# A four-layer graph network: group sums in four PSUM banks, turned rows stored from ScalarE's queue, x copied by rank beside the rank loop

## The chip, the cores and the metric

The kernel runs on 1 core of one Trainium2 chip. The time is device microseconds of one execution, as a median of runs. All numbers are fp32 unless said otherwise.

## The reference

50000 nodes with 128 features, 50000 edges sorted by `dst`. Four residual layers, each on `h = relu(layernorm(x))`:

```python
dst = (50000 * uniform ** 2.0), sorted        # a few nodes get many edges
# layer 0: two graph convolutions
h1 = relu(segsum((h * ns @ W1)[src], dst) * nd + b1)
x  = x + segsum((h1 * ns @ W2)[src], dst) * nd + b2
# layer 1: x + [h, mean_in(h)] @ W.T + b
# layer 2: SAGE: h4 = relu(h @ Ws1 + mean_in(h) @ Wn1 + b1); x + h4 @ Ws2 + mean_in(h4) @ Wn2 + b2
# layer 3: m = gelu([h[src], h[dst], ew] @ We1 + be1) @ We2 + be2
#          u = gelu([h, segsum(m, dst)] @ Wu1 + bu1) @ Wu2 + bu2; x + layernorm(h + u) * gamma + beta
```

`ns`, `nd` are roots of the degrees, `mean_in` is the mean over a node's incoming edges.

## The kernel before

**Setup.** The 50000 nodes are 392 blocks of 128, the edges 392 tiles of 128. A histogram gives degrees and the edges of each block. The blocks are ranked by rising number of edges; four ranks make a group, 98 groups. The rank loop (98 turns) places the edges by rank of their block: TensorE counts, VectorE reads out positions, GpSimd scatters four times a turn. Beside it the first layer's table is made: SyncE loads 512 rows of x into `XB` (`load0`), ScalarE norms them into `HO`, TensorE turns them, ScalarE copies them (`HT`), TensorE multiplies by W1, ScalarE copies the product (`T1`), SyncE stores it (`store0`).

**Walks.** Then come six walks over the edges (`walk(ph)`, ph 0 to 5), one for each segment sum. A walk has 784 steps in 98 windows of 8; a step multiplies one tile of gathered messages (`M`, a ring of 32 tiles of 128 rows, filled by GpSimd's indirect gathers, four tiles a chunk) with a one-hot matrix (`OH`, VectorE compares `lane` with `dstrel`) and adds it to the sums of one block in PSUM. Steps go on to the next block or the next tile, as the data has it; tables `tab_p` (TensorE: rows and sums of each step, banks to clear), `tab_a` (ScalarE: banks to copy and slots in `AG`) and `tab_w` (GpSimd: the window that frees a chunk) say which. The sums of three groups stand in banks 0 to 2. A window first clears the banks that become new (two matmuls by zero, also into unused banks 4 and 6 where none does), after ScalarE has copied the sums of the window before (`ev_act`). After a window ScalarE copies two banks to `AG`.

**Consumers.** Beside each walk the finished groups are processed, some windows later: rows scaled and x added (VectorE, `pre`), variance, deviation (ScalarE), scale and offset (`coefficients`), norm to `HO` (ScalarE), transposed by TensorE into `pt` (bank 3), copied to `HT`, multiplied (banks 4, 5 or 6, 7 by parity), copied to `T1`, the state added to `T2`, and both stored as the next walk's table and state. After walk 2 the turned rows are stored too (`h3_d`), after walk 4 (`h5_d`) as well; walk 3 has a two-layer network as its consumer. Walk 5 gathers by src and by dst from a table of pairs, makes the messages (gelu), stores them and loads them back in order, and its consumer makes the output. Walks 0 to 5 are the first to the sixth walk in the prediction.

**Order.** Each engine runs `staggered(...)`: in step n it does part (lag, do) for group n - lag, in the order of the list, so each list is the order written out by hand of one engine's queue. Waits block everything behind them in that list. The second convolution's x is needed in rank order: `placed1` (SyncE, walk 0) stores four blocks of the table and copies four blocks of x from DRAM to DRAM for each group. In code:

```python
staggered(sp, [(3, store0), (1, rows_for(s_ho))])                       # rank loop, SyncE
staggered(sp, [(5, placed1)])                                           # walk 0, SyncE
staggered(act, [(5, product(1)), (4, turned(1)), (3, normed(1, Z)), (0, sums(0))])
staggered(dve, [(0, onehots(1)), (4, coefficients(2, s_pre)), (6, added(2, ...)), (3, pre(2, ndr, b2bc))], chain, 4)
staggered(dve, [(0, onehots(2)), (4, coefficients(3, s_pre)), (3, pre(3, rdr, lbbc))], chain, 4)
```

`link` makes VectorE wait for its own last operation.

Of the kernel before, what the change touches and what calls it, by code (L numbers as in the profile page):

```python
# [57 lines left out]
class Chain:  # L58
# [15 lines left out]
    def link(self, ins):  # L74
        ins.then_inc(self.sem, 1)
        if self.i is None:
            self.done += 1
            self.eng.wait_ge(self.sem, self.done)
        else:
            self.k += 1  # L80
            self.eng.wait_ge(self.sem, self.i * self.per + (self.done - self.first * self.per + self.k))
# [27 lines left out]
def program(nc, a, out):  # L109
    with ExitStack() as ctx, ExitStack() as early:  # L110
# [32 lines left out]
        def four(t):  # L143
# [56 lines left out]
        bb_i = tmp("bb_i", [1, WINS], I32); b12_i = tmp("b12_i", [1, STEPS], I32); t16 = tmp("t16", [1, WINS], I32)  # L200
        b12_f = tmp("b12_f", [1, STEPS]); g_f = tmp("g_f", [1, WINS]); gk = tmp("gk", [1, 3, WINS]); gw = tmp("gw", [1, 3, WINS])
        g3_i = tmp("g3_i", [1, 3, WINS], I32); g3_f = tmp("g3_f", [1, 3, WINS]); moved = tmp("moved", [1, WINS]); spare = tmp("spare", [1, WINS]); fresh = tmp("fresh", [1, 2, WINS]); high = tmp("high", [1, WINS], I32)
        p_f = tmp("p_f", [1, STEPS]); m_f = tmp("m_f", [1, STEPS])
# [12 lines left out]
        AG = sb("AG", [P, AGR * W4])  # L216
# [8 lines left out]
        pt = ps[3]  # L225
# [16 lines left out]
        ev_act = sem("sums_copied")  # L242
# [6 lines left out]
        s_mma = sem("hidden_products"); s_hid = sem("hidden_made"); s_z6 = sem("updated_normed"); s_nrm = sem("updated_scaled"); s_fin = sem("output_made")  # L249
        s_es = sem("edges_summed"); s_gl = sem("messages_made")  # L250
        in_ = pair("rows_loaded"); late = pair("late_loaded")
        st = pair("table_stored"); sv = pair("state_stored"); sh = pair("turned_stored")
# [4 lines left out]
               "mma": [0, 0, 0, 0, 1, 0, 1], "hid": [0, 0, 0, 0, 1, 0, 1]}  # L257
        TURN = {"in": [64, 0, 32, 16, 16, 16, 32], "late": [0, 0, 0, 0, 16, 0, 16], "st": [16, 64, 64, 64, 64, 64, 64],
                "sv": [0, 64, 16, 16, 16, 16, 0], "sh": [0, 0, 0, 16, 0, 16, 0]}
# [36 lines left out]
        def half_of(d, b, k):  # L296

            if d == 4:
                return [ps[4 + 2 * h].rearrange("p (j k d) -> p j k d", j=2, k=2)[:, :, k, :] for h in range(2)]
            return [banks[:, (4 + 2 * b) * W4:(6 + 2 * b) * W4].rearrange("p (j k d) -> p j k d", j=Q4, k=2)[:, :, k, :]]  # L300
# [12 lines left out]
        def _(sp):  # L313
# [62 lines left out]

            staggered(sp, [(1, rows_for(s_var))])
# [11 lines left out]

            def spots(g):  # L390

                return entries(sp, tab_s[0:1, ds(g * Q4, Q4)], Q4, (BLOCKS - 1) * P)
# [11 lines left out]
            def whole_rows(d, table, buf, ready, done):  # L404

                def do(i, b):
                    g = 2 * i + b
                    sp.wait_ge(ready[0], g + (at(d, ready[1]) + 1))
                    stand(sp)
                    sp.dma_start(table[g], buf[:, b, :]).then_inc(done[b], 16)  # L410
# [16 lines left out]
            def placed1(i, b):  # L427
                g = 2 * i + b
                sp.wait_ge(s_t1, g + (at(1, "t1") + 1))
                stand(sp)  # L430
                to = spots(g)
                for j, r in enumerate(to):
                    sp.dma_start(tabs[1][ds(r, P), :], q(T1[:, b, :])[:, j, :]).then_inc(st[b], 16)
                for j, r in enumerate(to):
                    if isinstance(g, int) and g == GROUPS - 1 and j >= 2:
                        part = slice((j - 2) * (REST // 2), (j - 1) * (REST // 2))
                        sp.dma_start(q(x_rank[g])[part, 2, :], rest(2)[part]).then_inc(sv[b], 16)
                        continue
# [591 lines left out]
        def _(dve):  # L1030
# [305 lines left out]
            def pre(d, col, bias):  # L1336

                def do(i, b):
# [10 lines left out]
                    if d == 2:  # L1349
                        stand(dve)  # L1350
# [93 lines left out]
```

## Time and profile before

| | |
|---|---|
| median of 3 runs (lowest to highest) | 5862.01 us (5845.89 to 5865.06) |
| profiled execution | 5851.2 us, span 5849.4 us |
| granted TensorE clock, mean | 0.911 |
| busy: TensorE, VectorE, ScalarE, GpSimd | 4302.6, 3428.6, 3079.0, 3264.7 us |
| DMA | 879 MB, mean 150 GB/s |

Stages from the first gather or scatter of one to that of the next: setup to 441 us, rank loop to 1079, tables to 1157, then the walks to 1791, 2458, 3051, 4015, 4658 and the end. In rows of the profile PE is TensorE, PEld its weight loads, DVE VectorE, ACT ScalarE, POOL GpSimd, SP SyncE, `<-` names what ended an idle time. The clock is a share of the full 2.4 GHz. fp32 matmuls show two records each.

### The profile page before, as it was taken

The numbers are of one execution on the slowest core, as the hardware profiler recorded it, in microseconds if no ns is written. First come the engines' busy times: TensorE is split into PE (matmuls) and PEld (weight loads), VectorE is DVE, ScalarE is ACT, GpSimd is POOL, SyncE is SP. The second block draws the span as 40 slices with busy tenths as digits, with TensorE's granted clock in tenths as the row PEclk, the third lists the DMA queues.
The fourth block names the chain that finished last, engine by engine and source line by source line (L and its number), as shares of the span: only waits on it lengthen the run. The fifth ranks groups of instructions, "written<-read, shape, count | busy, mean of one in ns | idle before, by whom it ended". The sixth has DMA issues, their size and how long they took to land. (4 is left out here: it accounts for less than half of the span.)

```text
span 5849.4 us, 136722 instructions
## 1 busy us (share of the span) xinstructions
PE 4302.6 (74%) x23129; PEld 3083.8 (53%) x23130; DVE 3428.6 (59%) x11290; ACT 3079.0 (53%) x6571; POOL 3264.7 (56%) x3244
## 2 busy tenths in 40 slices
PE   4556666577766888666649999998888537777777
PEld 1123333265555666555537777776667425455554
DVE  6875555443335877688843333334777426666666
ACT  7954444155545666466633333334666416666667
POOL 0006555275775557676764333454667577777771
PEclk8879999699988999889869999999999769999998
DMA  2212333144444555477754444455888646666665
GB/s 76 75 50 77 81 83 80 42 122 123 131 125 130 154 158 165 138 242 235 240 153 129 132 134 134 142 149 157 252 254 262 188 117 188 188 194 189 187 190 146
DMA packets 1061001, 879.24 MB, mean 150 GB/s; under 512 B 134328, under 2 KB 866000, under 8 KB 1060924
## 3 DMA queue, kind: packets, MB, share of 16 engines
q1 hardware_dynamic: 960572, 697.60, 39.5%
q0 software_dynamic: 100352, 180.83, 12.0%
q14 instruction: 56, 0.46, 0.0%
q8 instruction: 21, 0.34, 0.0%
HBM read 491.13 MB, written 412.40 MB: 154 GB/s over the span
## 5 line engine op out<-in xcount | busy, mean ns | idle before, releaser
L965 PE MATMUL banks<-M,OH 128*128 x9408 | 1322.5, 300 | 291.8 <-POOLq L593 167.4
L564 POOL DMA_INDIRECT M<-table_a,six x1176 | 1244.1, 1058 | 520.6 <-issue 327.5
L965 PEld LDWEIGHTS banks<-M,OH 128*128 128x128 f32 x9408 | 1246.0, 211 | 460.9 <-issue 432.0
L564 POOL DMA_INDIRECT M<-table_b,six x784 | 787.4, 1004 | 728.3 <-PE banks L965 499.6
L653 ACT ACTIVATE AG<-banks x1176 | 633.6, 591 | 771.6 <-PE banks L965 765.3
L1311 DVE TENSOR_TENSOR OH<-lane,dstrel 128x1024 f32<-128x1024 f32 x588 | 719.9, 1225 | 479.0 <-PE banks L965 348.4
L559 POOL DMA_INDIRECT edges_by_block<-pack,pos_i x392 | 376.0, 959 | 690.5 <-DVE pos_i L1184 591.5
L956 PE MATMUL banks<-zero_h 128*128 128x512 f16 x1176 | 360.8, 389 | 411.9 <-issue 254.6
L653 ACT ACTIVATE T<-banks 128x512 f32<-128x512 f32 (+1 forms) x588 | 295.9, 520 | 534.9 <-DMA table_b<-T 229.3
L883 PE MATMUL banks<-ident,HO 128*128 128x128 f32 x2352 | 380.8, 286 | 210.8 <-ACT HO L670 173.7
L564 POOL DMA_INDIRECT M<-table_pairs,dix x392 | 446.9, 1140 | 119.5 <-issue 101.8
L564 POOL DMA_INDIRECT M<-table_pairs,six x392 | 377.5, 963 | 128.2 <-issue 114.0
L653 ACT ACTIVATE HT<-banks 128x512 f32<-128x512 f32 x686 | 407.0, 593 | 57.1 <-PE banks L883 50.2
L883 PEld LDWEIGHTS banks<-ident,HO 128*128 128x128 f32 x2352 | 280.4, 145 | 294.4 <-ACT HO L670 192.1
L956 PEld LDWEIGHTS banks<-zero_h 128*128 128x128 f16 x1176 | 114.1, 97 | 572.8 <-issue 548.6
L1361 DVE TENSOR_TENSOR T<-banks,XB 128x256 f32<-128x256 f32 x196 | 74.0, 419 | 566.5 <-ACT T L653 559.3
L1002 PE MATMUL banks<-w,H 128*128 128x256 f32 x1568 | 355.1, 380 | 5.9 <-ACT H L762 5.9
L674 ACT ACTIVATE HO<-Z,BI,SC 128x128 f32<-128x128 f32 x784 | 322.3, 483 | 64.9 <-DVE BI L1268 58.7
L1177 DVE CUSTOM_DVE_ANT_0 junk<-banks,oh_bk 128x392 f32<-128x392 f32 x392 | 220.2, 562 | 218.3 <-PE banks L871 213.7
L670 ACT ACTIVATE HO<-XB,dclamp,steps_c 128x128 f32<-128x128 f32 x392 | 161.3, 482 | 336.1 <-DMA XB<-in_x 322.8
L1392 DVE SCALAR_TENSOR_TENSOR ES<-we1c,ewT,M 128x128 f32<-128x128 f32 x392 | 111.6, 346 | 356.1 <-POOLq L593 295.8
L1002 PEld LDWEIGHTS banks<-w,H 128*128 128x128 f32 x1568 | 290.4, 190 | 44.6 <-ACT H L762 9.2
(270 smaller groups left out, 7795.8 us busy)
## 6 DMA issues: line engine op xcount, KB each, us to landing
XB<-state SPq DMA_DIRECT2D x392, 256.0 KB
state<-T SPq DMA_DIRECT2D x196, 256.0 KB
table_a<-T SPq DMA_DIRECT2D x784, 64.0 KB
state<-Z SPq DMA_DIRECT2D x196, 256.0 KB
h_turned<-HT SPq DMA_DIRECT2D x196, 256.0 KB
table_pairs<-T SPq DMA_DIRECT2D x392, 128.0 KB
M<-messages SPq DMA_DIRECT2D x98, 512.0 KB, 4.2
XB<-in_x SPq DMA_DIRECT2D x390, 128.0 KB
```

The lines of the kernel that those rows point to most:

```text
L559: nc.gpsimd.indirect_dma_start(out=edges, out_offset=bass.IndirectOffsetOnAxis(ap=pos_i[b][:, j:j + 1], axis=0), in_=pack[b][:, j, :], in_ ...
L564: nc.gpsimd.indirect_dma_start(out=M[:, slot, :], out_offset=None, in_=table, in_offset=bass.IndirectOffsetOnAxis(ap=idx, axis=0)).then_in ...
L653: return nc.scalar.activation(dst_, src_, ACT.Copy)
L670: last = nc.scalar.activation(q(HO[:, b, :])[:, j, :], cell, ACT.Relu, bias=bix[:, ds(g * Q4 + j, 1)], scale=scx[:, ds(g * Q4 + j, 1)])
L674: last = nc.scalar.activation(q(HO[:, b, :])[:, j, :], cell, ACT.Relu, bias=BI[:, b, j:j + 1], scale=SC[:, b, j:j + 1])
L883: last = nc.tensor.transpose(q(pt)[:, j, :], q(src_[:, b, :])[:, j, :], ident[:, :])
L956: mm(banks[:, ds(fresh_at[k], W4)], zero_h[:, 0:P], zero_h[:, :], start=True, stop=False, skip_group_check=True)
L965: last = mm(banks[:, ds(sums_at[k], P)], OH[:, b * US + k, :], source[:, ds(rows_at[k], P)], start=False, stop=False, skip_group_check=True)
L1002: last = mm(half, q(H[:, b, h, :])[:, j, :], w42[:, h, :, :].rearrange("p k d -> p (k d)"), start=(h == 0), stop=(h == 1))
L1177: v.tensor_tensor_reduce(junk[:, c % 2, :], ps[4 + c % 2][:, 0:BLOCKS], oh_bk[:, c, :], 1.0, 0.0, ALU.mult, ALU.add, posf[:, c:c + 1]).the ...
L1311: v.tensor_tensor(OH[:, b * US:(b + 1) * US, :], lanes, ids, ALU.is_equal).then_inc(oh_ready, 1)
L1392: last = v.scalar_tensor_tensor(q(ES[:, b, :])[:, j, :], we1c[:, :], ewT[:, ds(c * GC + j, 1)], M[:, b * GC + j, :], ALU.mult, ALU.add)
```

## The change

1. *Four banks.* Sums stand in banks 0 to 3. `tab_p` clears one bank ahead of a window and one ahead of its fifth step; the first clear waits for the copies of the window before the last, the second for the first copy of the last window (`ev_first`). `AG` gets a spare slot for copies that carry nothing. `pt` moves to bank 4, products to banks 5 and 6 for both parities, the fourth walk's to 7 and 4, and the wait `copied` of the walks goes.
2. *Constants in PSUM.* Bank 7 holds `lane` and the biases b1, b2 and that of layer 1; one-hots of walks 0, 1, 2 and 4 and the bias adds read them there.
3. *x by rank.* `by_rank` copies x in the rank loop, four blocks a turn; walk 0 has the table's stores alone.
4. *Turned rows* of walks 2 and 4 are stored from ScalarE's queue.
5. *VectorE's consumer* is split in six parts (`walked`), rows of walks 1, 2 and 4 are scaled into four slots (`Z4`), the bias is added a step before it is used.
6. *Walk 5.* ScalarE makes `T1`; norm, gamma and beta are 12 operations 128 wide on VectorE instead of ScalarE's four and VectorE's three 512 wide.
7. Other orders and lags in nearly every list, and shorter table arithmetic ahead of the walks.

```diff
-        pt = ps[3]
+        pt = ps[4]
+        lanes_p, b1_p, b2_p, lb_p = (ps[7][:, k * P:(k + 1) * P] for k in range(4))
 # SyncE
-            staggered(sp, [(3, store0), (1, rows_for(s_ho))])
+            def by_rank(i, b):
+                g = 2 * i + b
+                for j, r in enumerate(spots(g)):
...
+                    sp.dma_start(q(x_rank[g])[:, j, :], a["x"][ds(r, P), :]).then_inc(sx[b], 16)
+            staggered(sp, [(1, rows_for(s_ho)), (4, store0), (4, by_rank)])
-            staggered(sp, [(5, placed1)])
+            staggered(sp, [(0, placed(1, tabs[1], T1, (s_t1, "t1"), st))])
 # ScalarE
+                    act.dma_start(table[g], HT[:, b, :]).then_inc(sh[b], 16)
-                    copy(AG[:, ds(spot[2], W4)], banks[:, ds(spot[0], W4)])
+                    copy(AG[:, ds(spot[2], W4)], banks[:, ds(spot[0], W4)]).then_inc(ev_first, 1)
                     copy(AG[:, ds(spot[3], W4)], banks[:, ds(spot[1], W4)]).then_inc(ev_act, 1)
-            staggered(act, [(5, product(1)), (4, turned(1)), (3, normed(1, Z)), (0, sums(0))])
+            staggered(act, [(0, sums(0)), (2, turned(1)), (1, normed(1, Z)), (3, product(1))])
-            staggered(act, [(5, product(2)), (4, turned(2)), (3, normed(2, None)), (0, sums(1)), (2, deviations(...))])
+            staggered(act, [(4, normed(2, None)), (1, sums(1)), (4, turned(2)), (5, product(2)), (3, deviations(...))])
-            staggered(act, [(4, turned(3)), (3, normed(3, Z)), (0, sums(2)), (2, deviations(...))])
+            staggered(act, [(1, sums(2)), (3, deviations(...)), (5, turned(3)), (3, normed(3, None)), (5, turned_stored(3, h3_d))])
 # TensorE, products
-                    need(pe, s_t1, g + (at(d, "t1") - 1))
+                    need(pe, s_t1, g + at(d, "t1") - (1 if d < 2 else 0))
 # TensorE, walk
-                    need(pe, ev_act, w + WINS * ph)
-                    for k in range(2):
-                        mm(banks[:, ds(fresh_at[k], W4)], zero_h[:, 0:P], zero_h[:, :], ...)
+                    need(pe, ev_act, w + (WINS * ph - 1))
+                    mm(banks[:, ds(fresh_at[0], W4)], zero_h[:, 0:P], zero_h[:, :], ...)
...
                     for k in range(US):
+                        if k == US // 2:
+                            need(pe, ev_first, w + WINS * ph)
+                            mm(banks[:, ds(fresh_at[1], W4)], zero_h[:, 0:P], zero_h[:, :], ...)
-            staggered(pe, [(0, walk(3, copied(4, 5))), (4, out4), (2, turn_rows(4, HO)), (3, hidden4)])
+            staggered(pe, [(0, walk(3)), (2, turn_rows(4, HO)), (3, hidden4), (4, out4)])
 # VectorE
-                    lanes = lane[:, :]...
+                    lanes = (lanes_p if ph in (0, 1, 2, 4) else lane[:, :])...
-            staggered(dve, [(0, onehots(1)), (4, coefficients(2, s_pre)), (6, added(2, ...)), (3, pre(2, ndr, b2bc))], chain, 4)
+            staggered(dve, [(5, roots), (5, offsets), (4, summed_rows), (4, stats), (4, variances), (0, onehots(1)), (3, biased), (6, added(2, ...))], chain, 3)
-            staggered(dve, [(0, onehots(2)), (4, coefficients(3, s_pre)), (3, pre(3, rdr, lbbc))], chain, 4)
+            staggered(dve, [(4, summed_rows), (4, stats), (4, variances), (0, onehots(2)), (3, biased), (4, roots), (4, offsets)], chain, 3)
 # VectorE, final of walk 5
-                link(v.tensor_tensor(q(XB[:, b, :]), q(XB[:, b, :]), four(bet), ALU.add))
-                link(v.tensor_tensor(q(T2[:, b, :]), q(HO[:, b, :]), four(gam), ALU.mult))
-                v.tensor_tensor(T2[:, b, :], T2[:, b, :], XB[:, b, :], ALU.add).then_inc(s_fin, 1)
+                for j in range(Q4):
+                    v.tensor_tensor(q(XB[:, b, :])[:, j, :], q(XB[:, b, :])[:, j, :], bet[:, :], ALU.add)
+                for j in range(Q4):
+                    last = v.scalar_tensor_tensor(q(T2[:, b, :])[:, j, :], q(Z[:, b, :])[:, j, :], MV[:, b, j, 0:1], gam[:, :], ALU.subtract, ALU.mult)
+                for j in range(Q4):
+                    last = v.scalar_tensor_tensor(q(T2[:, b, :])[:, j, :], q(T2[:, b, :])[:, j, :], SC[:, b, j:j + 1], q(XB[:, b, :])[:, j, :], ALU.mult, ALU.add)
-            staggered(dve, [(0, edges6), (L + 6, updated), (L - 1, onehots(5)), (L + 7, coefficients(6, s_z6)), (L + 2, pre6), (L + 8, final)], chain, 6)
+            staggered(dve, [(0, edges6), (L + 6, updated), (L - 1, onehots(5)), (L + 7, final)], chain, 4)
```

## Rows read from the trace of the kernel before

**Rows 1.** Windows by stage: length, busy PE, PEld, DVE, ACT, POOL, clock, DMA, GB/s.

```profile
441.00:1079.00 638.00, 422.42 (x2338) 252.24 (x2337) 358.49 (x1552) 265.43 (x584) 376.02 (x392) 0.92 0.31 81
1157.00:1791.00 634.00, 444.88 (x2943) 356.94 (x2943) 229.41 (x489) 316.63 (x784) 419.45 (x405) 0.94 0.45 121
1791.00:2458.00 667.00, 522.72 (x2943) 423.86 (x2943) 510.38 (x1668) 388.28 (x882) 416.12 (x405) 0.92 0.52 155
2458.00:3051.00 593.00, 371.80 (x2159) 296.27 (x2159) 439.04 (x1567) 342.88 (x784) 416.70 (x405) 0.85 0.71 216
3051.00:4015.00 964.00, 942.47 (x4511) 682.92 (x4511) 316.50 (x490) 342.86 (x686) 380.91 (x405) 0.99 0.46 133
4015.00:4658.00 643.00, 504.70 (x2940) 416.80 (x2941) 449.86 (x1568) 386.77 (x882) 421.46 (x406) 0.93 0.80 240
4658.00:5850.00 1192.00, 826.04 (x4314) 557.67 (x4312) 745.20 (x2058) 705.41 (x1174) 828.75 (x808) 0.89 0.59 173
```

**Rows 2.** Windows, steady stretches of four walks, L965 alone (PE, PEld).

```profile
1250.00:1650.00 400.00, 138.76 (x1065) 126.12 (x1063) 0.99 0.48 128
1900.00:2400.00 500.00, 180.74 (x1216) 166.86 (x1216) 0.93 0.54 160
2500.00:2900.00 400.00, 180.53 (x1183) 166.32 (x1182) 0.91 0.78 238
4100.00:4500.00 400.00, 146.69 (x1047) 135.04 (x1048) 0.96 0.85 255
```

**Rows 3.** GpSimd's groups: busy, mean ns, idle before; first, second, third, fifth, sixth walk.

```profile
L564 POOL DMA_INDIRECT M<-table_a,six x392 | 414.4, 1057 | 180.2 <-issue 110.9 <-PE banks L965 57.3 <-POOL six L573 9.5
L564 POOL DMA_INDIRECT M<-table_b,six x392 | 409.9, 1046 | 220.3 <-issue 108.3 <-PE banks L965 103.0 <-POOL six L573 7.5
L564 POOL DMA_INDIRECT M<-table_a,six x392 | 412.3, 1052 | 155.3 <-issue 107.7 <-PE banks L965 30.6 <-POOL six L573 10.3
L564 POOL DMA_INDIRECT M<-table_a,six x392 | 417.4, 1065 | 185.1 <-issue 108.9 <-PE banks L965 63.8 <-POOL six L573 9.4
L564 POOL DMA_INDIRECT M<-table_pairs,dix x392 | 446.9, 1140 | 119.5 <-issue 101.8 <-DMA M<-table_pairs,dix 12.2 <-DMA M<-table_pairs,six 5.5
```

**Rows 4.** Timeline, three places: start us, length us, engine, instruction.

```profile
4309.88 1.22 DVE L1311 TENSOR_TENSOR OH<-lane,dstrel 128x1024 f32<-128x1024 f32 x1 [0.34 <-issue]
...
4310.02 1.90 POOL L564 DMA_INDIRECT M<-table_a,six  x1 [0.30 <-issue]
...
5209.66 0.67 DVE L1413 TENSOR_TENSOR XB<-XB,bet 128x512 f32<-128x512 f32 x1
...
5209.80 1.35 POOL L564 DMA_INDIRECT M<-table_pairs,dix  x1 [0.30 <-issue]
...
3507.62 0.76 DVE L1361 TENSOR_TENSOR T<-banks,XB 128x256 f32<-128x256 f32 x2 [6.15 <-ACT T L653]
3507.74 0.95 POOL L564 DMA_INDIRECT M<-table_b,six  x1 [0.30 <-issue]
```

**Rows 5.** Timeline of the rank loop and of SyncE's queue in the first walk.

```profile
763.07 0.93 SPq L366 DMA_DIRECT2D XB<-in_x  x2
...
766.70 1.65 ACT L670 ACTIVATE HO<-XB,dclamp,steps_c 128x128 f32<-128x128 f32 x4 [3.59 <-DMA XB<-in_x]
...
1604.56 2.90 SPq L440 DMA_DIRECT2D x_by_rank<-in_x  x4
```

**Rows 6.** Timeline of VectorE, one step of the second walk.

```profile
2105.05 1.23 DVE L1311 TENSOR_TENSOR OH<-lane,dstrel 128x1024 f32<-128x1024 f32 x1 [0.33 <-issue]
...
2106.79 0.69 DVE L1361 TENSOR_TENSOR T<-banks,H 128x512 f32<-128x512 f32 x1 [0.23 <-issue]
2107.40 0.72 DVE L1342 TENSOR_TENSOR XB<-XB,b2bc 128x512 f32<-128x512 f32 x1
2108.76 1.14 DVE L1323 SCALAR_TENSOR_TENSOR H<-AG,ndr,XB 128x128 f32 x4 [0.65 <-ACT HO L674]
...
2111.39 1.23 DVE L1311 TENSOR_TENSOR OH<-lane,dstrel 128x1024 f32<-128x1024 f32 x1
```

More of the change, by code:

```diff
@@ L77, in link, with made, after @@
             self.done += 1
[L78 to L81, printed above, removed]
+            return self.done
+        self.k += 1
+        return self.i, self.per, self.done - self.first * self.per + self.k
+    def made(self, less):
+        if self.i is None:
+            return self.done - less
+        return self.i, self.per, self.done - self.first * self.per + self.k - less
+    def after(self, mark):
+        if not isinstance(mark, int):
+            mark = mark[0] * mark[1] + mark[2]
+        self.eng.wait_ge(self.sem, mark)
+    def link(self, ins):
+        self.after(self.mark(ins))
 def staggered(eng, parts, chain=None, links=0):
@@ L425, in kept @@
                     sp.wait_ge(sems[k], turns(d + 1, what))
[L427 to L438, printed above, removed]
-                    r = nc.s_assert_within(r, 0, (FULL - 1) * P, skip_runtime_bounds_check_because="the last two ranks are the last two blocks")
-                    sp.dma_start(q(x_rank[g])[:, j, :], a["x"][ds(r, P), :]).then_inc(sv[b], 16)
-            staggered(sp, [(5, placed1)])
-            kept(1, "sv", sv)
+            staggered(sp, [(0, placed(1, tabs[1], T1, (s_t1, "t1"), st))])
+            for k in range(2):
+                sp.wait_ge(sx[k], 64 * TURNS)
             def load2(i, b):
                 g = 2 * i + b
-                need(sp, s_var, g + (at(2, "var") - 1))
+                need(sp, s_row, g + (at(2, "row") - 1))
                 stand(sp)
@@ L996, in out4 @@
                 pe.wait_ge(s_hid, g + (at(4, "hid") + 1))
+                pe.wait_ge(s_ht, g + (at(4, "ht") + 3) if not isinstance(g, int) else at(4, "ht") + min(g + 3, GROUPS))
                 need(pe, s_t1, g + at(4, "t1"))
@@ L1302, in _, with constants @@
             dve.wait_ge(s_tq, 17)
+            def constants():
+                for row, what in ((lanes_p, lane), (b1_p, b1bc), (b2_p, b2bc), (lb_p, lbbc)):
+                    last = v.tensor_copy(row, what[:, :])
+                link(last)
             def onehots(ph):
@@ L1345, in do @@
-                    if d in (3, 5):
-                        need(dve, sv[b], turns(d, "sv", i))
-                    into = Z4(i, b) if d == 2 else Z[:, b, :]
-                    link(scaled(i, b, col, lambda j: q(XB[:, b, :])[:, j, :], into))
-                    if d == 2:
-                        stand(dve)
-                    spread(d, b, into).then_inc(s_var, 1)
-                return do
+                    if bias is None:
+                        dve.wait_ge(in_[b], turns(d, "in", i) + TURN["in"][d])
+                    else:
+                        chain.after(chain.made(0 if isinstance(g, int) else 1))
```

293 lines of the change are left out of this document (153 added, 140 removed).

## The prediction

> **What bounds the kernel now.** I read the table of stages first, then the walks' own matmuls in steady stretches, then GpSimd's gathers, then single steps of the timeline. Outside the setup there are a rank loop and six walks; a walk is 98 windows of 8 steps [rows 1]. Only the fourth walk is full on one engine (TensorE 942 of 964 us). In the others TensorE is busy 372 to 523 us of 593 to 667, so I looked for what paces a window. Sixteen walk matmul records make a window, so a steady window takes 400 x 16 / 1065 = 6.0 us in the first walk, 6.6 in the second, 5.4 in the third and 6.1 in the fifth [rows 2].
>
> GpSimd gathers 392 tiles a walk. A gather that nothing delays takes 0.945 us and the next starts 0.30 later; with some 13 us of table reads, c = 1.26 us a tile. The rows show means of 1.05 to 1.07 and waits for TensorE (the ring of 32 tiles is full) of 57, 103, 31 and 64 us [rows 3]. The timeline shows what lengthens a gather: one that starts 0.14 us into the one-hot comparison ends 0.8 us after the comparison does, 1.90 us in all; the same happens with the 512-wide add of beta; a gather that starts inside an add whose first operand is in PSUM takes 0.95 [rows 4]. The excess over 0.945 is 392 x 0.112 = 44 us in the first walk, 40, 42 and 47 in the second, third and fifth [rows 3].
>
> Both matter because of the data. dst is 50000 u squared and the blocks stand in rising order of edges, so light blocks come first: after w windows N = 392 (1 - v) tiles are used, v = (sqrt(9 - 4w/49) - 1) / 2. Demand rises from 2.7 to 8 tiles a window. A walk at p us a window and c us a tile ends at T = the largest over w of p w + c (360 - N), and not before 98 p or 392 c. Check on before: third walk (p 5.41, c 1.37) 556, fifth (6.1, 1.37) 600, first (6.0, 1.35) 594; the stages are 593, 643 and 634 long [rows 1], so filling and draining add 37 to 43. Where I forecast a walk, the difference of two such T is the gain.
>
> **The change, part by part.** *Rank loop.* Today SyncE's store waits for ScalarE's T copy and stands ahead of the next load, so the load of x is issued at 763.07 and the rows are normed at 766.70, and ScalarE had waited 3.6 us for it; a group takes 638 / 98 = 6.5 us [rows 1, 5]. After, the load stands first and the store lags by 4. The wait falls away, but SyncE gets four copies of x: 2.90 us [rows 5]. Its sum a group: loads 0.93, copies 2.90, and for one store, the gaps and the table read some 1.7: 5.5. GpSimd's four scatters take 4 x 1.26 = 5.0. I take 5.6, and 98 x 0.9 = 88, less 8 for start: **-80**. Bounds: -10 (copies and loads share the queue, the loads land late) and -105 (5.3). Transfers have room: DMA is at 0.31 there.
>
> *Table arithmetic on VectorE* ahead of the walks: 14 us of short one-row operations become some 8: **-6**.
>
> *First walk.* SyncE issues four stores and four x copies a window, 1.9 and 2.9 us plus 1.1 of gaps, which is the 6.0 of the window [rows 2, 5]. The copies leave. What is next: TensorE's own work, 445 / 98 = 4.5 us [rows 1]; the copy of the sums, which held the bank clears, now has a window's slack through the fourth bank and the second half's own wait. I take p = 4.8. One-hot lanes and the bias are read from PSUM, so by rows 4 no gather is delayed: c = 1.26. T = 501 against 594, and two lags less to drain, 8 us: **-102**. Bounds: p 5.5 gives 545, -50; all at GpSimd's 392 x 1.26 = 494 gives -110.
>
> *Second walk.* VectorE is the pace: from one comparison to the next 6.34 us, in it 0.65 us before the scaled rows, spent on ScalarE's norm of two groups back and on register work behind the bias add [rows 6]. Four H slots and the bias add taken a step ahead remove the wait, some 0.25 of register work stays: 5.94. TensorE needs 523 / 98 = 5.3. Products(g) now also wait for both T copies of g - 1. Counted from the start of VectorE's step: those products end at 2.4, ScalarE copies them behind its norm (1.65), sums (1.05) and turned copy (0.6) by 4.3, VectorE adds last in its step by 5.9, and TensorE wants the bank at 6.6: 0.7 to spare. p = 5.94 and c = 1.28 (scaled rows still read two SBUF operands, but 128 wide, about 10 us a walk) give T = 583; before it was 667 less 36 for filling and draining, 631: **-48**. Bounds: 0 and -85 (5.4).
>
> *Third walk.* VectorE's step has the same gap, 5.4 becomes 5.3 (a semaphore wait is added ahead of the statistics, 0.12). ScalarE gets the store of the turned rows, about 0.5 us in its queue behind 343 / 98 = 3.5 busy [rows 1]; SyncE loses as much. c from 1.37 to 1.28: T 556 to 535: **-21**. Bounds: +10, -45.
>
> *Fourth walk.* TensorE is full (942 of 964 us); clears, transposes and products are as many as before. It now needs T copies 2.6 us after the last product; they end at about 1.8. **0**; bounds +30, -10.
>
> *Fifth walk.* VectorE busy 450 / 98 = 4.6, TensorE 5.15, so 6.1 is waits (stores of the pair table, ScalarE's norm) that the new order relaxes. But DMA is at 0.85 in the steady stretch [rows 2]; at 5.6 us it would be 0.93. p = 5.6, c = 1.28: 555 against 600: **-45**. Bounds: 0 and -65.
>
> *Sixth walk.* GpSimd has 784 gathers and is never free; the second four of a window take 1.140 in the mean [rows 3]. 392 x 0.195 = 76 us of delay, most of it under two 512-wide operations with both operands in SBUF. They become 128 wide, twelve instead of three, and a gather then waits for one short operation, 0.15 us in the mean instead of 0.4: -40. The drain after the last gather stays on TensorE and loses a lag and ScalarE's norm: -5. **-45**. Bounds: -10, -75. The one-hots here still read SBUF.
>
> The constants in PSUM cost nothing by the rows: the 512-wide add from PSUM takes 0.69 us, the one from SBUF 0.72 [rows 6]; copying them twice takes 3 us.
>
> Two rules bear on this. The Trainium skill (SBUF, section Who interferes with whom) says that a VectorE instruction with two SBUF inputs contends with a GpSimd instruction that reads SBUF; by that rule, too, the excess goes, and the trace agrees (1.90 against 0.95 us). Against the change speaks the Trainium skill (VectorE: DVE Perf Modes, section on the TRN2 errata): its table gives a PSUM source 120 fixed cycles and an SBUF source 58, an estimate of 0.065 us more an operation, 6 us a walk for each of the seven moved to PSUM, so up to 45 us less gain. The trace does not agree: 0.69 us from PSUM, 0.72 from SBUF [rows 6].
>
> **Sum.** 80 + 6 + 102 + 48 + 21 + 0 + 45 + 45 = 347. The profiled execution took 5851.2 us (span 5849.4), the median of the runs is 5862 and the lowest 5846: 5851 - 347 = 5504, and as a median **5508**.
>
> **Rivals.**
> A, *every walk but the fourth becomes GpSimd's*: the waits for a full ring go to nothing (103 and 64 us in the second and fifth walk). For: GpSimd's rows show it close behind everywhere. Against: VectorE's step of 5.3 to 5.9 has work of 5.2 in it. The second, third and fifth walk gain 85, 45 and 65 instead of 114 together: 5508 - 81 = 5427, with the rank loop at its bound 5400.
> B, *the steps stay serial*: orders and lags move the waits, each walk keeps p and only c falls; the rank loop's loads queue behind the x copies. Then first walk -50, third -15, second and fifth -5 each, sixth -40, rank -25, table -6: -146, 5705. For: the second walk's 0.65 us wait is half register work. Against: x copies leave SyncE whatever else happens.
> C, *slower*: products in one pair of banks. Products of g wait for the add of g - 1, which stands last in VectorE's step. If TensorE's products end after that place is reached, the step runs round products, copy, add: 1.9 + 0.7 + 0.7 + the rest of VectorE's 5.2 = 8.5 us a window in the second and fifth walk. 196 x 2.7 = 529 more than forecast: 6037. It decides once the copy comes more than some 2.5 us later in the step than now; my count has 0.7 of slack for TensorE, so only partly.
> D, *gathers don't get shorter*: a PSUM operand saves nothing because the instruction's other operand or its write holds GpSimd. c stays 1.35 and 1.37: the first walk gains 28 less, the second 7, third 13, fifth 12, sixth 40: 5608. Against: rows 4.
>
> **Chances.** Forecast 0.50; A 0.17; B 0.17; D 0.08; C 0.04; the rest, 0.04, is mixtures near before. The range takes in A (5400) and most of B: 5390 to 5690. A measurement can tell 0.3%, some 18 us, from no change. Faster 0.93, same 0.02, slower 0.05.
>
> **What would show it.** Rank loop 5.6 us a group, ScalarE's wait for x near nothing. Steady windows of 4.8, 5.9, 5.3, 9.6, 5.6 us. Mean gather 0.95 in the first walk and 0.96 to 0.98 in the second, third and fifth, 1.03 for the second four of the sixth. Stages of about 532, 619, 572, 964, 598 and 1147 us. It is wrong if the comparison reading PSUM is longer than 1.23 us, if VectorE's add waits on ScalarE's copy in the second walk (C), or if SyncE in the rank loop holds the loads back (B).

## The result and the profile after

The changed kernel takes 5635.58 us in the median (5630.41 to 5637.73, 4 runs), the kernel before beside it 5856.97 (5845.89 to 5865.06): ratio 0.9622, 95% interval 0.9603 to 0.9641. The profiled execution has a span of 5634.9 us for 5849.4. The forecast was 5508; of the 347 us that its terms add up to, 221 came.

The table of stages after answers to [rows 1], in the same order. The lengths are set from the gathers' starts.

```profile
441.00:1004.00 563.00, 384.74 (x2325) 232.94 (x2323) 354.52 (x1552) 261.82 (x577) 375.67 (x391) 0.99 0.49 133
1082.00:1617.00 535.00, 415.08 (x2942) 361.47 (x2942) 221.90 (x492) 327.01 (x784) 373.39 (x406) 0.91 0.36 97
1617.00:2278.00 661.00, 538.56 (x2942) 445.37 (x2942) 493.55 (x1666) 384.04 (x882) 375.35 (x405) 0.89 0.53 155
2278.00:2860.00 582.00, 392.52 (x2158) 312.42 (x2158) 432.95 (x1568) 341.81 (x784) 375.04 (x405) 0.86 0.73 221
2860.00:3829.00 969.00, 943.74 (x4510) 697.04 (x4510) 326.76 (x494) 343.17 (x686) 427.79 (x405) 0.99 0.46 133
3829.00:4491.00 662.00, 521.10 (x2941) 435.00 (x2941) 434.02 (x1570) 384.04 (x882) 375.39 (x406) 0.91 0.78 233
4491.00:5635.00 1144.00, 830.36 (x4314) 571.55 (x4312) 776.60 (x2744) 610.64 (x880) 780.38 (x808) 0.88 0.62 180
```

| stage, us | before | forecast | after | difference |
|---|---|---|---|---|
| rank loop and tables | 715 | 629 | 641 | -75 |
| first walk | 635 | 532 | 535 | -100 |
| second walk | 667 | 619 | 661 | -5 |
| third walk | 594 | 572 | 582 | -12 |
| fourth walk | 964 | 964 | 969 | +5 |
| fifth walk | 643 | 598 | 662 | +20 |
| sixth walk | 1191 | 1147 | 1143 | -48 |

So rank loop, first and sixth walk came near their forecast lengths, and the second, third and fifth did not. It isn't the gathers. GpSimd's groups of the first, second, third, fifth and sixth walk, which answer to [rows 3]:

```profile
L575 POOL DMA_INDIRECT M<-table_a,six x392 | 370.6, 945 | 139.4 <-issue 110.5 <-PE banks L987 17.3 <-POOL six L584 7.6
L575 POOL DMA_INDIRECT M<-table_b,six x392 | 372.4, 950 | 250.5 <-PE banks L987 134.3 <-issue 105.7 <-POOL six L584 8.4
L575 POOL DMA_INDIRECT M<-table_a,six x392 | 372.1, 949 | 185.4 <-issue 108.8 <-PE banks L987 61.7 <-POOL six L584 9.4
L575 POOL DMA_INDIRECT M<-table_a,six x392 | 372.2, 949 | 252.3 <-PE banks L987 137.4 <-issue 104.4 <-POOL six L584 7.5
L575 POOL DMA_INDIRECT M<-table_pairs,dix x392 | 396.9, 1013 | 119.5 <-issue 99.7 <-DMA M<-table_pairs,dix 12.8 <-DMA M<-table_pairs,six 7.0
```

Every walk whose one-hots read PSUM has its gathers at 0.945 to 0.950 us, but in the second, third and fifth the time saved stands as longer waits for the ring (134, 62 and 137 us, for 103, 31 and 64 before): something downstream has not become faster. The windows of L987, the walk's own matmuls, say the same. Here they are for the first, second, third and fifth walk: 400 x 16 / 1248 = 5.1 us a window (6.0 before, 4.8 forecast), 6.5 (6.6), 5.5 (5.4), 6.5 (6.1) [rows 2].

```profile
1150.00:1550.00 400.00, 181.97 (x1248) 167.44 (x1248) 0.95 0.38 102
1700.00:2200.00 500.00, 200.41 (x1232) 189.93 (x1232) 0.91 0.55 160
2350.00:2750.00 400.00, 199.26 (x1163) 177.49 (x1162) 0.91 0.77 235
3850.00:4350.00 500.00, 196.44 (x1235) 186.16 (x1234) 0.92 0.79 237
```

In the rank loop SyncE is never idle for long: 0.97 + 0.41 + 2.98 us of issues and 1.4 of gaps and table reads make a group of 5.77 us (5.5 counted, 5.6 taken). This is SyncE's queue:

```profile
636.25 0.97 SPq L380 DMA_DIRECT2D XB<-in_x  x2
637.59 0.41 SPq L389 DMA_DIRECT2D table_a<-T  x1
638.67 2.98 SPq L407 DMA_DIRECT2D x_by_rank<-in_x  x4
642.02 0.96 SPq L380 DMA_DIRECT2D XB<-in_x  x2
```

ScalarE still waits for the load of x, nearly as long as before. These are its rows in the rank loop before (638 us of it) and after (544 us); columns: us in total, times, longest.

```profile
ACT HO L670 <- DMA XB<-in_x: 322.8, 96, 5.6
```

```profile
ACT HO L681 <- DMA XB<-in_x: 236.7, 87, 3.8
```

Then the second walk. First what TensorE waited for in 580 us of it, before and (second fence) after; columns: who, for what, us in total, times, longest.

```profile
PE banks L956 <- issue: 80.5, 56, 1.8
PE banks L956 <- ACT AG L653: 9.0, 10, 1.0
PE banks L883 <- ACT HO L674: 8.3, 34, 0.3
```

```profile
PE banks L975 <- issue: 73.2, 45, 1.7
PE banks L905 <- ACT HO L685: 10.1, 32, 0.4
```

TensorE was busy 469.9 of those 580 us before and 485.3 after. Of what is left, 80.5 and 73.2 us is the row "issue", in which no other engine holds it, and only 17.3 and 10.1 is a wait for ScalarE. So TensorE was full with its own queue, before and after. The row "issue" ahead of the first clear is the load of the window's 16 table words, which the transposes stand in front of:

```profile
L968 PEldq TENSOR_LOAD <-tab_p x588: 1101/1196/2312, 1079.4 to 5570.6; - x196
```

It takes 1.1 us at least. TensorE's timeline after shows when it costs:

```profile
1901.40 1.05 PE L987 MATMUL banks<-M,OH 128*128 x8
1902.29 0.38 PE L986 MATMUL banks<-zero_h 128*128 128x512 f16 x1
1902.50 1.05 PE L987 MATMUL banks<-M,OH 128*128 x8
1903.62 1.99 PE L923 MATMUL banks<-wlT,HT 128*128 128x256 f32 x8
1905.93 0.65 PE L905 MATMUL banks<-ident,HO 128*128 128x128 f32 x4 [0.32 <-ACT HO L685]
1908.17 0.38 PE L975 MATMUL banks<-zero_h 128*128 128x512 f16 x1 [1.59 <-issue]
1908.70 1.85 PE L987 MATMUL banks<-M,OH 128*128 x8
...
1910.77 1.83 PE L987 MATMUL banks<-M,OH 128*128 x8
```

The transposes wait 0.3 us for ScalarE's norm, and the queue behind them stands. So the load begins only at 1906.48, behind them, takes 1.40 us, and TensorE idles 1.6 us. The eight matmul records behind that hole take 1.85 us where they took 1.05: the granted clock from 1908.7 to 1912.4 is 0.54, from 1901.4 to 1903.6 it is 1.00 (the two levels are 1.2 and 2.4 GHz). In the next window nothing waits, a load of 1.50 us runs from 1911.62 under the queued matmuls, and there is no hole.

### The profile page after: what moved, and what is told of

Its sections match the earlier page's. It is cut to its first block and busy times, and to the rows that moved or that the text cites. A ratio compares the mean times of both kernels' runs of the same rounds, so it can differ in the third digit from the quotient of the medians.

```text
span 5634.9 us, 137799 instructions
## 1 busy us (share of the span) xinstructions
PE 4293.6 (76%) x23123; PEld 3153.7 (56%) x23124; DVE 3413.1 (61%) x11963; ACT 2986.5 (53%) x6277; POOL 3088.3 (55%) x3244
## 5 line engine op out<-in xcount | busy, mean ns | idle before, releaser
L987 PE MATMUL banks<-M,OH 128*128 x9408 | 1442.9, 302 | 277.5 <-POOLq L604 131.3
L987 PEld LDWEIGHTS banks<-M,OH 128*128 128x128 f32 x9408 | 1366.5, 212 | 443.7 <-issue 388.6
L575 POOL DMA_INDIRECT M<-table_a,six x1176 | 1114.8, 948 | 577.0 <-issue 323.7
L685 ACT ACTIVATE HO<-H,BI,SC 128x128 f32 (+1 forms) x1176 | 484.1, 482 | 418.3 <-DVE BI L1347 390.1
L1307 DVE TENSOR_TENSOR OH<-banks,dstrel 128x1024 f32<-128x1024 f32 x392 | 478.4, 1221 | 78.4 <-PE banks L987 60.2
L575 POOL DMA_INDIRECT M<-table_pairs,dix x392 | 396.9, 1013 | 119.5 <-issue 99.7
L975 PE MATMUL banks<-zero_h 128*128 128x512 f16 x588 | 229.9, 391 | 292.2 <-issue 243.0
L1319 DVE SCALAR_TENSOR_TENSOR H<-AG,rdr,XB 128x128 f32 (+1 forms) x784 | 225.1, 348 | 238.7 <-DMA XB<-state 115.8
L1319 DVE SCALAR_TENSOR_TENSOR Z<-AG,ndr,banks 128x128 f32<-128x128 f32 x392 | 109.8, 342 | 291.2 <-ACT AG L664 291.2
```

Source lines behind the costliest of these rows:

```text
L575: nc.gpsimd.indirect_dma_start(out=M[:, slot, :], out_offset=None, in_=table, in_offset=bass.IndirectOffsetOnAxis(ap=idx, axis=0)).then_in ...
L685: last = nc.scalar.activation(q(HO[:, b, :])[:, j, :], cell, ACT.Relu, bias=BI[:, b, j:j + 1], scale=SC[:, b, j:j + 1])
L975: mm(banks[:, ds(fresh_at[0], W4)], zero_h[:, 0:P], zero_h[:, :], start=True, stop=False, skip_group_check=True)
L987: last = mm(banks[:, ds(sums_at[k], P)], OH[:, b * US + k, :], source[:, ds(rows_at[k], P)], start=False, stop=False, skip_group_check=True)
L1307: v.tensor_tensor(OH[:, b * US:(b + 1) * US, :], lanes, ids, ALU.is_equal).then_inc(oh_ready, 1)
L1319: last = v.scalar_tensor_tensor(q(into)[:, j, :], q(sums_at)[:, j, :], col[:, ds(g * Q4 + j, 1)], other(j), ALU.mult, ALU.add)
```

## The experiments

Each run is one kernel made from the changed one. The stages below go from the first gather of a walk to that of the next, each read from one trace. Stages that a run leaves alone show what differs from run to run: the second walk, untouched, took 657 to 665 us in seven of them, the fifth 662 to 672 in six.

| run | kernel us | rank | 1 | 2 | 3 | 4 | 5 | 6 |
|---|---|---|---|---|---|---|---|---|
| changed | 5635.6 | 641 | 535 | 661 | 582 | 969 | 662 | 1143 |
| e1 product first | 5640.9 | 640 | 536 | 656 | 582 | 968 | 684 | 1144 |
| e2 constants SBUF | 5728.7 | 640 | 600 | 678 | 600 | 969 | 662 | 1138 |
| e3 x beside walk 1 | 5684.7 | 565 | 657 | 665 | 583 | 969 | 671 | 1142 |
| e4 turned by sync | 5685.1 | 642 | 536 | 657 | 637 | 969 | 654 | 1145 |
| e5 transposes later | 5576.7 | 642 | 536 | 608 | 581 | 968 | 653 | 1147 |
| e6 one-hots last | 5624.4 | 642 | 536 | 664 | 568 | 968 | 671 | 1140 |
| e7 x copies shared | 5571.6 | 571 | 536 | 660 | 580 | 968 | 668 | 1141 |
| e8 beta wide | 5642.4 | 640 | 536 | 658 | 583 | 967 | 672 | 1144 |
| e9 combined | 5447.3 | 571 | 536 | 615 | 555 | 969 | 610 | 1144 |
| e10 output wide | 5638.2 | 642 | 535 | 665 | 582 | 968 | 666 | 1140 |

**e1, the product's copy first.**

```
-[(4, normed(2, None)), (1, sums(1)), (4, turned(2)), (5, product(2)), (3, deviations...)]
+[(4, normed(2, None)), (5, product(2)), (1, sums(1)), (4, turned(2)), (3, deviations...)]   (fifth walk likewise)
```

> The changed kernel with ScalarE's list altered in the second and fifth walk: the copy of the product stands right behind the norm, ahead of the copies of the sums and of the turned rows. Theory 1, the ring through the single pair of product banks (norm, transposes, turned copy, product copy, VectorE's add, next products) paces these two walks: the copy comes about 1.7 us earlier in a step, a steady window falls from 6.5 to 6.0 us in each, the stages from 661 and 662 to about 620 each, the kernel to about 5555. Theory 2, the pace is the loop from VectorE's statistics through ScalarE's root and norm, or TensorE at half clock: the copy's place means nothing, both stages stay within 10 us, the kernel 5620 to 5650. Theory 3, the copies of the sums now come later and hold the bank clears: stages 10 to 30 us longer.

The second walk stayed (656), the fifth grew by 22, 12 more than the longest untouched one. The ring through the single pair of product banks (rival C) doesn't pace them; in 600 us of the fifth, ScalarE now waited 139 us for the products, and the sums behind them held the first clear for 59.

**e2, constants from SBUF.**

```
-lanes = (lanes_p if ph in (0, 1, 2, 4) else lane[:, :])...   b1_p, b2_p, lb_p
+lanes = lane[:, :]...                                        b1bc, b2bc, lbbc
```

> The changed kernel with the one-hot lanes and the three biases read from SBUF again. Theory 1, shorter gathers carry much of the first walk: its mean gather returns to 1.05 us, its stage from 535 to about 555; the second, third and fifth walk also have gathers of 1.04 to 1.06 but wait for other things, so each gets at most 10 us longer; kernel 5650 to 5680. Rival, only the pace of the windows counts and GpSimd's ring absorbs the delays everywhere: no stage moves by over 8 us, kernel within 0.3% of 5636. Rival, reading PSUM itself costs VectorE time: the second, third and fifth walk get shorter.

The first walk's mean gather rose to 1.134 us, more than before's 1.057, and the stage by 65. About as many gathers start under a one-hot as before (93 for 89), but they start earlier in it (0.38 us after its start in the mean, 0.64 before), so they wait longer for its end. The second and third walk lost 16 and 18, the fifth nothing. That is more than any of the three expectations had (kernel 5650 to 5680, first walk 555). The constants in PSUM, lanes and biases together, carry 93 of the 221 us.

**e3, x copied beside the first walk.**

```
-staggered(sp, [(1, rows_for(s_ho)), (4, store0), (4, by_rank)])
+staggered(sp, [(1, rows_for(s_ho)), (4, store0)])
-staggered(sp, [(0, placed(1, ...))])
+staggered(sp, [(0, placed(1, ...)), (1, by_rank)])
```

> The changed kernel with the copies of x by rank taken out of the rank loop and put behind the four table stores in the first walk, as before. Theory 1, SyncE's queue sets both stages: the rank loop falls from 5.8 us a group to GpSimd's 5.0 to 5.3 (563 to about 510 us from first to last scatter), the first walk returns to 6.0 us a window (stage 535 to about 615 to 630), kernel 5670 to 5690. Rival, the rank loop is paced by VectorE and TensorE: it stays at 5.8, kernel 5720 or more. Rival, the first walk gained from the fourth bank and the reordered slots: it stays under 560, kernel 5590 to 5630.

Both halves of the theory hold in direction: the rank loop gets 76 us shorter, the first walk 122 longer, more than expected (657 for 615 to 630). In the first walk neither the fourth bank nor the short gathers show while SyncE has four stores and four copies to issue: 657, no less than the 635 before. Moving the copies was worth 49 us.

**e4, turned rows stored by SyncE.**

```
-act: (5, turned_stored(3, h3_d))        (4, turned_stored(5, h5_d))
+sp:  (4, whole_rows(3, h3_d, HT, ...))  (3, whole_rows(5, h5_d, HT, ...))
```

> The changed kernel with the store of the turned rows issued by SyncE again in the third and fifth walk (ahead of the table stores of its step in the third, ahead of the pair stores in the fifth), as before. Theory 1, SyncE's queue is the late one in the fifth walk (the state load is issued up to 3.8 us too late): with 0.45 us more a step the fifth stage grows from 662 to 680 or more and the third by 10. Theory 2, ScalarE's queue is the scarce one (its norm follows BI at once and its copies hold others): taking 0.5 us off it shortens the fifth to about 640 and the third by 10 or more. Neither: both within 8 us, kernel within 0.3% of 5636.

The third walk takes 55 us more, the fifth 8 to 18 less. In the fifth the store is thus not what makes SyncE late. In the third the run doesn't separate the queue from the place: the store stands ahead of the table stores and the load of state rows, and its lag of 4 is one less than that of ScalarE's copy of the turned rows. In 580 us of that walk SyncE waited 117 us for this copy, and VectorE has a row that it doesn't have in the changed kernel:

```profile
DVE XB L1351 <- DMA XB<-state: 62.7, 47, 1.9
```

So the store at this place in SyncE's list costs 55 us. What it would cost one step later or behind the load was not run.

**e5, transposes and products one group later.**

```
pe   (4, products(2, ..)), (3, turn_rows(2, HO))  ->  (5, products(2, ..)), (4, turn_rows(2, HO))
act  (1, sums(1)), (4, turned(2)), (5, product(2)) -> (6, product(2)), (1, sums(1)), (5, turned(2))
dve  (6, added(2, ..)) -> (7, added(2, ..))        fifth walk likewise; SyncE's stores one later
```

> The changed kernel with TensorE's transposes and products one group later in the second and fifth walk (lags 4 and 5 for 3 and 4), the copies, the add and the stores that follow them one group later too, and the product's copy ahead of the sums. The transposes then never wait for the norm. Theory 3, TensorE is the pace there: at every other window its transposes wait for the norm, so the load of the 16 table words behind them (1.4 to 1.7 us) is not covered by queued matmuls, and after that hole a whole walk runs at half clock. Then the wait before the first clear (73 and 79 us in all) nearly goes, walks return to 2.2 us, a window falls to 5.6 to 5.9, the stages from 661 and 662 to 590 to 620 each: kernel 5540 to 5580. Rival, VectorE's step of 5.9 to 6.1 takes over at once: 10 to 25 us a stage, kernel near 5600. Rival, the hole moves to another place: kernel within 0.3% of 5636.

The second walk fell from 661 to 608. TensorE's waits in it over 540 us, and the stage windows of the second and fifth walk:

```profile
PE banks L923 <- DVE T L1388: 29.8, 79, 0.6
PE banks L987 <- POOLq L604: 18.3, 7, 4.8
PE banks L987 <- issue: 7.0, 38, 0.2
PE banks L975 <- issue: 2.8, 13, 0.3
```

```profile
1618.00:2226.00 608.00, 519.13 (x2942) 420.13 (x2942) 490.36 (x1666) 391.18 (x882) 374.72 (x405) 0.97 0.57 169
3774.00:4427.00 653.00, 516.77 (x2939) 420.60 (x2939) 433.47 (x1572) 396.97 (x882) 375.25 (x405) 0.97 0.79 236
```

The hole went (73 us in 580 to 3 in 540), the granted clock rose from 0.89 to 0.97, and the same 2942 matmul records took 19 us less. The edit also takes the product's copy forward, which gained nothing by itself in e1. So the hole was the cost of both. The window then is 5.8 us, VectorE's step: TensorE waits for its add. That is what the forecast had said for the pace (5.94), one obstacle later. The fifth walk lost its hole too (3 us left) and gained only 9 to 19 us, for here VectorE waited: its first two waits in 580 us of that walk.

```profile
DVE H L1319 <- DMA XB<-state: 100.8, 62, 3.6
DVE H L1319 <- ACT HO L685: 45.5, 21, 2.5
```

**e6, one-hots last in the third walk.**

```
-(4, variances), (0, onehots(2)), (3, biased), (4, roots), (4, offsets)
+(4, variances), (3, biased), (4, roots), (4, offsets), (0, onehots(2))
```

> The changed kernel with VectorE's list in the third walk as scaled rows, statistics, variances, bias add, reciprocal, BI, one-hots (the one-hots were before the bias add). Theory, VectorE is the pace of this walk: 5.0 us of work and 0.75 us of register instructions that begin only behind the reciprocal's own wait. With 1.2 us of one-hots behind that wait they are covered and BI comes 1.9 us earlier: a window falls from 5.5 to 5.0 us, the stage from 582 to 535 to 550, kernel 5590 to 5605. Rival, ScalarE's root isn't ready behind the bias add (0.7 us), and VectorE waits for it what it gains: stage within 10 us.

In 530 us of the changed kernel's third walk VectorE has this row. It is register instructions, which start only when the queue's wait for VectorE's own reciprocal is over:

```profile
DVE H L1319 <- issue: 69.4, 93, 1.1
```

In e6 the row is gone and the stage 14 us shorter (568), a third of what was expected: VectorE now waits 36 us for ScalarE's root and 22 for the state rows, as the rival had it. TensorE has the hole of the table load in this walk too, and larger than before: 78.4 us in 530 (65 times) for 48.4, and 68.0 in 520 in e6. No run filled it there, so which of the two holds the window at 5.5 us is not shown.

**e7, x copies shared.**

```
+act: (4, by_rank2)      blocks 2 and 3 of a group; SyncE keeps blocks 0 and 1
```

> The changed kernel with two of the four copies of x of a group issued by ScalarE instead of SyncE in the rank loop. Theory, SyncE's queue (5.8 us of issues a group) is the pace of the loop and GpSimd's four scatters (5.0) the next: first to last scatter from 564 to 490 to 510 us, and unlike with the copies in the first walk that stage stays at 535: kernel 5565 to 5585. Rival, ScalarE's norms now come late behind its own issues and table reads: 530 to 560, kernel 5600 to 5630.

From first to last scatter 503.5 us for 563.8, 5.1 a group: GpSimd's pace. The first walk stays at 536, as in the theory. 64 us in the median.

**e8, e10, wide operations in the sixth walk.**

```
e8:  four 128-wide adds of beta -> v.tensor_tensor(q(XB[:, b, :]), q(XB[:, b, :]), four(bet), ALU.add)
e10: four 128-wide (T2 * SC + XB) -> two 512-wide, T2 * SC and T2 + XB
```

> The changed kernel with the four 128-wide adds of beta in the sixth walk as one 512-wide add again. Theory, a gather that starts inside such an add waits for its end: mean gather of the second four from 1.013 up to 1.05 to 1.08, stage from 1143 to 1160 to 1175, kernel 5650 to 5665. Rival, the sixth walk gained from the norm taken off ScalarE and the lag less: stage within 5 us.

> The changed kernel with the last four 128-wide operations of the sixth walk's output (scale, add) as two 512-wide ones with both operands in SBUF, the same 1.4 us of work. Theory, the sixth walk's gain is its gathers' (GpSimd is never free there): gathers that start inside the wide ones wait up to 0.69 us, the mean of the second four rises from 1.013 to 1.05 to 1.10 and the stage from 1143 by 392 times that rise, 15 to 35 us: kernel 5650 to 5670. Rival, the gain came from the norm taken off ScalarE or from the order: stage within 5 us though the gathers lengthen. If the gathers don't meet these operations (as they didn't meet the wide add of beta), nothing moves.

Nothing moved in either, not even the mean gather (1.009 and 1.011 us). The gathers start at the same few places of VectorE's step in nearly every window. In the kernel before, 82 start in the wide add of beta and 82 in the wide last add, at 1.34 us in the mean: 64 us of excess over 0.945. In the changed kernel 83 start among the operations by gamma, at 1.09 us (12 us of excess), 83 start 0.03 us into one of the last four and take 0.944, and none starts in the adds of beta. So e8's wide add is met by no gather, and in e10 83 gathers start 0.56 us into a wide operation of 0.69 and take 0.945. The operations by gamma, the ones that gathers do meet, were made wide in no run.

**e9, the combination.**

```
e5 + e6 + e7, and
dve  (7, added(..)) ahead of onehots in the second and fifth walk
act  (1, loaded5) behind normed(5): the state rows of the fifth walk, loaded by ScalarE
sp   (4, whole_rows(5, h5_d, HT, ..)): its turned rows stored by SyncE; rows5 waits for its own last store
```

> The changed kernel with the edits that shortened a stage together (transposes and products a group later in the second and fifth walk, one-hots last in the third, two of four copies of x issued by ScalarE), and three more: VectorE's add of the product ahead of the one-hots in the second and fifth walk, there the load of the state rows issued by ScalarE behind its norm and the store of the turned rows by SyncE. If the stages are independent: rank loop 503, third walk 568, and the second at most 608. Theory, with TensorE's hole filled the products wait for VectorE's add (30 us in the second walk, 80 in the fifth) and in the fifth VectorE for the state rows, which SyncE issues behind the pair stores (101 us): the second walk falls to 575 to 600, the fifth from 653 to 590 to 620, kernel 5400 to 5450. Rival, ScalarE's queue becomes late in the fifth walk: 640 or more, kernel 5460 to 5480.

5447.25 us (5443.98 to 5451.22), ratio to before 0.9307, interval 0.9292 to 0.9323: it beats both kernels. The fifth walk fell to 610 as expected (the wait for state rows is gone from its list), the second got nothing from the earlier add (615 against 608, where 575 to 600 was expected; TensorE waits 70 us for the sums, which stand behind ScalarE's norm). The third took 555 for 568 with the same edit; why isn't known.

**e11 and e12.** Both are e9 with ScalarE's norm of the second walk behind the sums; in the sixth walk the adds of beta stand behind the operations by gamma, four 128-wide ones in e11, one 512-wide in e12.

> The combined kernel with two edits. In the second walk ScalarE copies the product and the sums ahead of its norm: TensorE waited there 70 us at the second clear for the sums. Theory: that wait goes, the walk takes 580 to 600 for 615 us. Rival: the norm comes 1.7 us later and the transposes wait for it, 610 or more. In the sixth walk the 128-wide operations by gamma stand ahead of the 128-wide adds of beta: a gather starts 2.35 us after the one-hots do, in the first of these adds, and waits at most 0.15 us for it: stage 1140 to 1150 as before, kernel 5410 to 5450.

> The kernel of the run before this one with the four 128-wide adds of beta as one 512-wide add at that place, 2.3 to 3.0 us after the one-hots' start, where a gather starts in each window. Theory, what a wide operation costs hangs on whether a gather starts inside it: this time it does, the gather waits 0.4 to 0.5 us, the mean of the second four rises by 0.08 to 0.12 us and the sixth stage by 30 to 45 us against the run before, all other stages equal. Rival, a wide operation costs nothing anywhere in this walk (two places cost nothing so far): within 5 us.

Beside these two the kernel before took 7018.2 us itself, and their own stages, setup apart, were longer than e9's, so these times (7000.86, ratio 0.9978, 0.9944 to 1.0012; and 7011.10, 0.9992) stand beside no other run, and the second walk's edit is not settled. What a gather does inside an add can be read all the same, first in e11, then in e12:

```profile
6479.43 0.88 DVE L1471 TENSOR_TENSOR XB<-XB,bet 128x128 f32<-128x128 f32 x4
6479.51 1.62 POOL L581 DMA_INDIRECT M<-table_pairs,dix  x1 [0.30 <-issue]
```

```profile
6040.64 0.69 DVE L1470 TENSOR_TENSOR XB<-XB,bet 128x512 f32<-128x512 f32 x1
6040.73 1.41 POOL L581 DMA_INDIRECT M<-table_pairs,dix  x1 [0.30 <-issue]
```

The gather ends 0.82 us after the last of the four adds (6480.31) and 0.81 after the wide one. Four short adds in a row hold it to the end of all four, 0.88 us, longer than the wide one, 0.69. This is no single case: the 57 gathers that start in e11's adds take 1.61 us in the mean, the 50 in e12's wide add 1.40. In the changed kernel a gather meets the operations by gamma, which have a scalar operand more, and there it gets in after the one that it started in, the second of four: 1.09 us.

```profile
5002.89 1.13 DVE L1446 SCALAR_TENSOR_TENSOR T<-Z,MV,gam 128x128 f32<-128x128 f32 x4
5003.20 1.28 ACT L794 ACT_TABLE_LOAD   x1
5003.22 1.09 POOL L575 DMA_INDIRECT M<-table_pairs,dix  x1 [0.30 <-issue]
```

## Why the prediction came out as it did

The measured time lies in the range, 128 us above the forecast and 54 below its upper end. It does so in part by luck: the range was drawn to take in most of B, in which the walks keep their pace. The second, third and fifth did keep it or lost some, but what held the second and the fifth stands in no rival.

*Rank loop and tables, -86 forecast, -75 measured.* The pace was right: SyncE's queue (e3, e7), 5.77 us a group for 5.6. But "the wait falls away" was wrong, and so was its sign, ScalarE's wait for x near nothing: it waits 2.7 us a time (236.7 / 87) for 3.4 before (322.8 / 96), as the load comes only as often as SyncE's queue turns. That costs nothing, because ScalarE isn't the pace.

*First walk, -102 and -100.* Both halves were needed, and each is shown alone: without the move of the copies the stage is 657 (e3), without the constants in PSUM 600 (e2). The agreement to 2 us hides two misses. A steady window is 5.1 us, not 4.8, and from its first matmul to its last the walk takes 510 us where T was 501 (597 and 594 before); filling and draining fell from 38 to 25 us where 8 less was booked. The c of 1.35 for this walk before is also low by the prediction's own rows, 1.26 + 0.112 = 1.37; T is 592 with the one and 594 with the other. (The second walk's bound has a slip of the same size: p = 5.4 gives T = 541, so -90 and not -85.)

*Second walk, -48 and -5: the step that failed.* The prediction had "VectorE is the pace" and "TensorE needs 523 / 98 = 5.3", from TensorE's busy time. It left out the hole of the table load, 80.5 us in 580, which stood among TensorE's waits before the change: with it TensorE was full at 6.6 us a window, and at 6.5 after. Relieving VectorE moved its own wait elsewhere. The prediction looked for C in the add that waits for the copy; that wait was there (58 us in 580, 42 times, up to 2.0), but as an effect, for e1 took the copy forward and gained nothing. So this sign of being wrong, which the prediction had named, appeared without the mechanism C that it stood for. e5 filled the hole and took the stage from 661 to 608, 59 below the kernel before, all that the term had promised and a little more, with the pace where the term had put it.

*Third walk, -21 and -12.* The term had VectorE's gap shrink; it moved from behind the bias add to behind BI and grew to 69.4 / 93 = 0.75 us, and the window stayed at 5.5. e6 got 14 us back by taking it away. TensorE's own hole grew here too (78.4 us in 530 for 48.4) and was in no term; its share is open. The store of the turned rows costs 55 us at the place in SyncE's list where e4 puts it, which the term had at nothing.

*Fifth walk, -45 and +20: the same step failed, and a second.* The hole before was 68 us in 550. And SyncE's list puts the pair stores, which wait for VectorE's last operation, ahead of the next load of state rows; the prediction had counted the stores of the pair table among the waits "that the new order relaxes", while the rows show VectorE waiting 108 us in 600 for these loads. Filling the hole alone gave 653 (e5). No run repaired the load alone: e4 (654) only moved the store of the turned rows, and VectorE still waited 111.4 us in 580 for state rows. Hole, loads, that store and the earlier add together gave 610 (e9), near the 598 forecast. Which part of that is whose was not separated. Memory traffic as the bound is out: e9 runs the same stretch at a DMA share of 0.88.

*Sixth walk, -45 and -48: right in size, in good part by luck.* The mean gather of the second four fell from 1.140 to 1.013 us, 392 x 0.127 = 50 us, which fits the stage's 48 if GpSimd is the pace here, as the prediction has it; no run tests that. The reason given was that a gather waits for a short operation, 0.15 us, instead of a wide one. That is what the 83 gathers among the operations by gamma do (1.09 us). But for beta and the last operations it isn't the width: e8 and e10 bring wide ones back for nothing, and e11 shows four short adds holding a gather longer than a wide one. The gathers no longer start inside those adds, because the operations around them went or moved. What wide operations by gamma would cost is not shown.

*Gathers.* 0.945 to 0.950 us where 0.95 to 0.98 was forecast, which decides against D. The Trainium skill (SBUF — State Buffer, section Who interferes with whom) puts the contention on VectorE instructions with two SBUF inputs; the trace agrees, and e2 shows it: 1.134 us in the first walk with lanes and bias in SBUF, 0.945 with them in PSUM. The price of a PSUM source in the Trainium skill (VectorE: DVE Perf Modes, section on the TRN2 errata) doesn't show: the one-hots take 1.221 us from PSUM and 1.225 from SBUF.

A (all walks GpSimd's) did not happen: the ring's waits grew. B (5705) was nearest in the second, third and fifth walk, as the steps there did stay serial, in the second and fifth by TensorE's own queue and in the fifth by the loads of state rows too.

## What to carry to other kernels

Before an engine is called free, add to its busy time what its own row "issue" says in the list of waits: in these walks a register load in its queue costs nothing while matmuls are queued ahead of it, and its full length once anything ahead of it waits, even 0.3 us. So put the instruction that may wait one group later, or put long queued work between it and the load. And an operation that another engine has to wait for is judged by what starts inside it, not by its width: look at the timeline where the starts fall.

## What the hardware showed that was not expected

- After a hole of 1.6 us on TensorE the walk's matmuls took 1.85 us for eight records where they took 1.05, at a granted clock of 0.54 for 1.00. With the holes filled the second walk's granted clock was 0.97 for 0.89 (e5).
- Short VectorE adds in a row, each with two SBUF operands and each starting before the last has ended (four in 0.88 us), hold a gather to the end of the row, 57 times in e11. Operations that take a scalar per row too (four in 1.13 us) let it in after the one that it met, 83 times in the changed kernel (1.09 us).
- On VectorE the register instructions of the next item take 0.75 us in the mean, up to 1.1, when the queue has just waited for the engine's own result; with the one-hots behind that wait the row is gone (e6).
